# Decoder layer with 64 experts: the shared expert in eleven chunks of rows, and experts and shared expert in one program without a barrier between them

## The reference, cut to what matters

```
logits = x @ gate_weight.T;  topk_w, topk_i = top 6 of 64 experts, from the best 3 of 8 groups
slot   = expert * 192 + position in the expert          # 192 places per expert
g, u   = buf @ Wg.T, buf @ Wu.T                         # 64 experts, 352 inner rows each
yk     = ((silu(g) * u) @ Wd.T)[slot]                   # six rows per token
routed = sum over k of topk_w[k] * yk[k]
shared = (silu(x @ Sg.T) * (x @ Su.T)) @ Sd.T           # 704 inner rows, all tokens
out    = x3 + routed + shared                           # x3: the stream before this block
```

## Time and profile before

| | |
|---|---|
| three runs | 1631.30, 1635.71, 1635.98 us; median 1635.71 us |
| profiled execution | 1641.41 us, span 1639.7 us |
| PE | 1506.2 us busy, 92% of the span |
| DVE, ACT, POOL | 70%, 55%, 47% of the span |
| mean granted clock of PE | 0.957 |
| self and cross attention | up to 670 us |
| expert phase | 670 to 1396 us |
| shared phase | 1396 to 1639.7 us |

### The profile page before, as it was taken

The page is one execution under the profiler, slowest core; times in us unless marked ns, Lnnn a source line. Parts: engine busy times, 40 slices in busy tenths (PEclk is TensorE's granted clock), DMA queues, the critical chain, the costliest instruction groups (busy, mean ns, idle before and its releaser), DMA issues. The chain is left out here.

```text
span 1639.7 us, 30631 instructions
## 1 busy us (share of the span) xinstructions
PE 1506.2 (92%) x10424; PEld 1248.8 (76%) x10424; DVE 1139.9 (70%) x2051; ACT 896.2 (55%) x1765; POOL 766.0 (47%) x957
## 2 busy tenths in 40 slices
PE   4999998989999865499999999999999998799997
PEld 3788886778888754388888888888888886676775
DVE  5677666546888787587777777777777774465655
ACT  3556665644544331287777777777777775312110
POOL 1122234233465555265655565556555653345543
PEclk9999998999999976599999999999999999799999
DMA  6012212321221110698877777788777772436553
GB/s 192 8 59 78 66 47 73 103 75 66 72 76 40 43 49 33 229 328 286 279 265 273 264 267 263 266 282 281 268 272 264 269 263 90 145 117 205 180 165 115
DMA packets 108609, 275.35 MB, mean 168 GB/s; under 512 B 16048, under 2 KB 16048, under 8 KB 108528
## 3 DMA queue, kind: packets, MB, share of 16 engines
q1 hardware_dynamic: 90784, 223.40, 40.2%
q0 software_dynamic: 15360, 50.34, 9.5%
q10 hardware_dynamic: 2384, 0.53, 0.2%
HBM read 232.28 MB, written 41.94 MB: 167 GB/s over the span
## 5 line engine op out<-in xcount | busy, mean ns | idle before, releaser
L2126 POOL TENSOR_TENSOR e_hid<-e_h_raw,e_hid 128x128 fp32r<-128x128 f32 (+1 forms) x192 | 163.9, 854 | 221.3 <-ACT e_hid L2192 221.3
L2350 PE MATMUL e_gu<-e_xT_hi_lo,e_wg 128*128 128x384 f32 (+1 forms) x768 | 231.4, 357 | 1.6 <-issue 1.6
L2350 PE MATMUL e_gu<-e_xT_hi_lo,e_wu 128*128 128x384 f32 (+1 forms) x768 | 230.3, 355 | 0.0
L2352 PE MATMUL e_gu<-e_xT_hi_lo,e_wu 128*128 128x192 f32 (+1 forms) x768 | 193.2, 252 | 0.0
L2352 PE MATMUL e_gu<-e_xT_hi_lo,e_wg 128*128 128x192 f32 (+1 forms) x768 | 193.0, 251 | 0.0
L2134 POOL TENSOR_TENSOR e_wd<-e_raw_d,e_wd 96x512 fp32r<-96x512 f32 x64 | 131.5, 2054 | 36.4 <-ACT e_wd L2177 36.4
L2263 DVE TENSOR_TENSOR e_total<-e_gu,e_low 128x384 f32<-128x384 f32 (+1 forms) x192 | 105.6, 550 | 54.5 <-issue 36.6
L2350 PEld LDWEIGHTS e_gu<-e_xT_hi_lo,e_wg 128*128 128x128 f32 (+1 forms) x768 | 138.0, 180 | 6.9 <-issue 2.6
L2352 PEld LDWEIGHTS e_gu<-e_xT_hi_lo,e_wg 128*128 128x128 f32 (+1 forms) x768 | 139.8, 182 | 1.4
L2350 PEld LDWEIGHTS e_gu<-e_xT_hi_lo,e_wu 128*128 128x128 f32 (+1 forms) x768 | 137.8, 179 | 3.8
L2352 PEld LDWEIGHTS e_gu<-e_xT_hi_lo,e_wu 128*128 128x128 f32 (+1 forms) x768 | 139.6, 182 | 0.0
(11 more groups left out here) (330 smaller groups left out, 4091.2 us busy)
## 6 DMA issues: line engine op xcount, KB each, us to landing
e_raw_g<-in_L_ffn_Wg_dram SPq DMA_DIRECT2D x64, 704.0 KB
e_raw_u<-in_L_ffn_Wu_dram SPq DMA_DIRECT2D x64, 704.0 KB
e_raw_d<-in_L_ffn_Wd_dram SPq DMA_DIRECT2D x64, 512.0 KB, 6.2
y_dram<-e_y_main SPq DMA_DIRECT2D x64, 256.0 KB, 7.9
e_raw_d<-in_L_ffn_Wd_dram SPq DMA_DIRECT2D x64, 192.0 KB, 7.5
y_dram<-e_y_rest SPq DMA_DIRECT2D x64, 128.0 KB, 7.0
a_v<-in_x_dram SPq DMA_DIRECT2D x16, 256.0 KB
s_xr<-in_x_dram SPq DMA_DIRECT2D x16, 256.0 KB
```

The costliest lines, as they stand in the source:

```text
L2126: pool.tensor_tensor(hid[b][1][0:n, c, :], h_raw[g.odd][b][0:n, c, 0:P], hid[b][0][0:n, c, :].bitcast(F32), ALU.subtract).then_inc(s_hl, 1)
L2350: pe.matmul(bank[0:n, 0:2 * CAP], w[b][0][:, k, m:m + n], xT[:, :, k, toks], start=k == 0, stop=False)
L2352: ins = pe.matmul(bank[0:n, 0:CAP], w[b][1][:, k, m:m + n], xT[:, 0, k, toks], start=False, stop=k == KC - 1)
```

## The change

Five things are changed, all in the expert and shared phases.

1. **Chunks.** The 704 inner rows become five full chunks of 128 and one half of 64 (`FULL = 5`, `HALF = 64`). In the sixth chunk the last 64 rows of gate and of up lie side by side in one weight buffer (`h_sg`, 768 columns wide), so that one set of 4 x `matmul3` makes both, gate in rows 0 to 63 of the bank and up in rows 64 to 127. There are 11 such sets instead of 12.
2. **Down.** The hidden values of the half chunk are kept as one buffer, lo part in rows 0 to 63 and hi part in rows 64 to 127; the weights of down likewise. Two matmuls then do what three did: per tile 17 instead of 18.
3. **Wait of down.** For the first tile of a quad, `down` waits chunk by chunk instead of for all.
4. **One program.** `expert_phase` and `shared_phase` become builders of five functions each, and `feed_forward` runs them one behind the other in one block. The barrier, and SP's wait for the last stores, are gone; instead POOL waits for the three stores before its first gather, and other instructions wait for the semaphore that frees their buffer or bank (`free`). The shared expert's buffers lie over expert buffers that are done: the lo weights over the raw ones (in place), the hi weights over the raw buffers of the experts.
5. **Work moved into the last turn.** `load_xf(0)` is issued in the first turn, behind the loads of the shared weights. The splits of the weights of gate and up (11 pieces of 128x512 instead of 8 of 128x704, in the order of use) and of the first tokens go between the last turn's instructions on ACT and DVE, the first 16 transposes between those of PE.

The core of the diff:

```diff
-SCH = ((0, 128), (128, 128), (256, 128), (384, 128), (512, 96), (608, 96))
+FULL = MS // P
+HALF = MS - FULL * P
+SCN = FULL + 1
+INNER = 2 * FULL + 1
@@ expert program, SP
+            ahead.load_xf(sp, 0)
@@ expert program, ACT, in half()
                 if more:
                     gu_hi(*nxt(g, b), 0)
+                else:
+                    ahead.split_hi(act, 0, 2)
...
+                else:
+                    ahead.split_hi(act, 2, 4)
...
-            for b in range(2):
-                main_out(pair(turns - 1), b)
+            ahead.x_hi(act, 0, 0, 2)
+            ahead.split_hi(act, 4, 6)
+            main_out(pair(turns - 1), 0)
+            ahead.x_hi(act, 0, 2, QT)
+            ahead.split_hi(act, 6, INNER)
+            main_out(pair(turns - 1), 1)
@@ expert program, DVE, behind the last half
+            ahead.x_lo(dve, 0, 0, 2)
+            ahead.split_lo(dve, 4, 6)
+            ahead.x_lo(dve, 0, 2, QT)
+            ahead.split_lo(dve, 6, INNER)
             rest_out(pair(turns - 1))
@@ expert program, PE
+                else:
+                    ahead.turn_tokens(pe, 0, 0, 2)
                 down_main(g, 0)
...
+            ahead.turn_tokens(pe, 0, 2, QT)
             down_main(pair(turns - 1), 1)
             down_rest(pair(turns - 1))
@@ shared program, POOL
+            for stored in free["y_stored"]:
+                pool.wait_ge(*stored)
@@ shared program, PE
             def hidden(q, first):
                 pe.wait_ge(s_tl, QT * (q + 1))
-                for c, (m, n) in enumerate(SCH):
+                if first:
+                    pe.wait_ge(*free["gate_up_banks"])
+                for c in range(SCN):
+                    if first:
+                        pe.wait_ge(s_wl, min(2 * c + 2, INNER))
...
-                    for w, bank in ((sg, gt[c % 2]), (su, up[c % 2])):
+                    for w, bank in ((sg, gt[c % 2]), (su, up[c % 2]))[0:2 if c < FULL else 1]:
...
             def down(q, first):
-                pe.wait_ge(s_hl, len(SCH) * (q + 1))
...
+                    for c in range(FULL):
+                        if t == 0:
+                            pe.wait_ge(s_hl, SCN * q + c + 1)
+                        matmul3(pe, bank[:], (hid[0][:, c, toks], hid[1][:, c, toks]), (sd[0][:, c, :], sd[1][:, c, :]),
+                                c == 0, False)
+                    if t == 0:
+                        pe.wait_ge(s_hl, SCN * (q + 1))
+                    pe.matmul(bank[:], hid_half[:, toks], sd[1][:, FULL, :], start=False, stop=False)
+                    pe.matmul(bank[:], hid_half[high_rows, toks], sd[0][high_rows, FULL, :], start=False, stop=True
+                              ).then_inc(s_dn, 1)
@@ feed_forward, one block
+        @block.tensor
+        def _(pe):
+            experts.pe(pe)
+            shared.pe(pe)
```

More of the change, by code:

```diff
@@ L2404, in _, with shared_buffers, sb, shared_programs @@
             turn(pair(turns - 1), False, True)
+            ahead.turn_tokens(pe, 0, 2, QT)
             down_main(pair(turns - 1), 1)
             down_rest(pair(turns - 1))
-def shared_phase(nc, raw, loaded, xf, x3, y_in, out, weight, slot, ident):
+        mine.sync, mine.pool, mine.act, mine.dve, mine.pe = sync, gpsimd, scalar, vector, tensor
+    return mine
+def shared_buffers(nc, ctx):
+    def sb(name, shape, dt=F32):
+        return ctx.enter_context(nc.sbuf_tensor("h_" + name, shape, dt))
+    return dict(xf=sb("xf", [P, QT, H]), ones=sb("ones", [P, 1]),
+                idx=[sb(f"idx{b}", [P, TOPK], U32) for b in range(2)], w_t=[sb(f"w_t{b}", [P, TOPK]) for b in range(2)],
+                carry=[sb(f"carry{b}", [P, 1]) for b in range(2)])
+def shared_programs(nc, sems, mine, own, raw, loaded, xf, x3, y_in, out, weight, slot, ident, experts):
     quads = BATCH // QT
@@ L2620, in turn @@
                         routed(q, early, range(3 * ((c - 1) % 2), 3 * ((c - 1) % 2) + 3))
-                hidden_lo(q, len(SCH) - 1, first)
+                hidden_lo(q, FULL, first)
                 if not last:
-                    x_lo(q + 1)
+                    x_lo(dve, q + 1, 0, QT)
                 for t in range(QT):
@@ L2691, in _, with feed_forward @@
             turn(quads - 1, False, True)
+        mine.load_xf, mine.split_hi, mine.split_lo = load_xf, split_hi, split_lo
+        mine.x_hi, mine.x_lo, mine.turn_tokens = x_hi, x_lo, turn_tokens
+        mine.sync, mine.pool, mine.act, mine.dve, mine.pe = sync, gpsimd, scalar, vector, tensor
+def feed_forward(nc, wg_in, wu_in, wd_in, shared_in, xf, x3, table, y, out, weight, slot, ident):
+    with ExitStack() as ctx:
+        sems = []
+        raw = []
+        own = shared_buffers(nc, ctx)
+        loaded = nc.alloc_semaphore("shared_weights_loaded")
+        sems.append(loaded)
+        shared = Programs()
+        experts = expert_programs(nc, sems, wg_in, wu_in, wd_in, xf, table, y, ident, shared_in, raw, loaded, shared)
+        shared_programs(nc, sems, shared, own, raw, loaded, xf, x3, y, out, weight, slot, ident, experts)
+        ctx.callback(end_phase, nc, sems)
+        block = ctx.enter_context(nc.Block())
+        @block.sync
+        def _(sp):
+            experts.sync(sp)
+            shared.sync(sp)
+        @block.gpsimd
+        def _(pool):
+            experts.pool(pool)
+            shared.pool(pool)
+        @block.scalar
+        def _(act):
+            experts.act(act)
+            shared.act(act)
+        @block.vector
+        def _(dve):
+            experts.dve(dve)
+            shared.dve(dve)
+        @block.tensor
+        def _(pe):
+            experts.pe(pe)
+            shared.pe(pe)
 _INS = ['x', 'ctx_2048', 'mask_BxS2_ik0', 'L0_attn_Wqkv', 'L0_attn_bqkv', 'L0_attn_Wo', 'L0_attn_bo', 'L0_xattn_Wq',
```

276 lines of the change are left out of this document (146 added, 130 removed).

## The result

| | before | after |
|---|---|---|
| median of four runs each, same chip | 1635.85 us | 1609.32 us (1608.08 to 1611.85) |
| ratio | | 0.9839, interval [0.9806, 0.9871] |
| profiled execution | 1641.41 us, span 1639.7 | 1611.85 us, span 1610.2 |
| TensorE's mean granted clock | 0.957 | 0.963 |

What follows compares the result with a forecast made beforehand. PE bounds the expert turns and nearly all of the shared phase, with a break between them. Terms 16.25 + 2.5 + 11.7 + 1.8 - 1.6 + 4.85 = 35.5 us give 1600.2, stated as 1600.5; range 1595 to 1609 (0.8).

Steps and rivals of the forecast that it cites:

- The seam: From the experts' last gate_up to the first shared-expert matmul: that matmul starts at 1391.5 instead of 1407.75, saving 16.25 us.
- the clock in quad 0: Start of quad 0: the first 12 matmuls run at clock 1.00 instead of 0.50, saving 2.5 us.
- 1.5 us that the text had kept for the range: In the seam: extra gain if the clock does not fall during down_main and down_rest; left out of the sum.
- Eleven chunks: Gate and up of each quad: 36 matmuls replace 48 in the last chunks, saving 2.93 us a quad, 11.7 in four.
- Down: Down stage: one matmul less per tile saves 0.92 us a quad, counting in quads 1 and 2, 1.8 us.
- The short last chunk: End of gate and up: DVE gives x_lo later, PE waits 0.8 us longer in quads 1 and 2, -1.6 us.
- Quad 1's wait for DVE: In quad 1: PE comes earlier and its wait for DVE grows from 0.95 to 1.9 us.
- The last quad: Quad 3: down begins on ready chunks, finish of tile 1 8.1 us after the last silu instead of 12.95; 4.85 us.
- The tail behind it stays: After finish of tile 1 in the last quad: the last routed sums and store, 14.9 us, remain unchanged.
- The start: Turn 1 of the experts: 1 MB loaded ahead of its weights costs 0, bounds 0 and 3.2 us.
- The first (clock and ACT give some back, 1603 to 1608): Quad 1 and start: falling clock, late silu and late weights cost 2 to 7 us; chance 0.20.
- Its rule from the Trainium skill: Quad 1's loop: branches to unheld instructions wait for a fetch, so late silus return in looping programs; sum then 1602.

Runs made afterwards that it cites:

- full_rows: The changed kernel with the half chunk's second down matmul on 128 rows, the lower 64 of its weights zero; 1607.24 us, 0.9826 of before.
- unrolled: all_quads with the loops over the quads written out on PE, ACT and DVE; 1593.85 us, 0.9737 of before.
- all_quads: combined with the token transposes behind the first two down tiles in quad 0 too; 1590.14 us, 0.972 of before.
- before_64: The kernel before with its inner rows cut as five chunks of 128 and one of 64, nothing else; 1636.39 us, 0.9983 of before.
- trios_early: The changed kernel with the groups of three routed sums behind chunks 0 to 3 instead of 1 to 4; 1605.36 us, 0.98 of before.
- x3_first: The changed kernel with SP asking for residual rows before it stores the output tile; 1608.56 us, 0.9805 of before.
- combined: The changed kernel with zero-padded half-chunk down, earlier routed sums, residual rows first, transposes behind down tiles in quads 1 and 2; 1594.27 us, 0.973.
- nothing_moved: The changed kernel with the shared expert's splits and token transposes behind the experts' last instructions, still one program; 1624.67 us, 0.9918 of before.

## Why the prediction was right in sign and 9 us short

- **The seam (16.25; measured 16.9) and the clock in quad 0 (2.5).** Right, with their mechanism: `h_gt` at 1389.70, no wait above 1.25 in the last turn, `hidden` of quad 0 30.1 us (1389.70 to 1419.76) where 29.9 were named. That the size came so near is in part luck. The clock stayed up through `down_main` and `e_dn_rest`, 1.5 us that the text had kept for the range. And the second `down_main` started 6.7 us behind `gate_up`'s end instead of 5.7, waiting for POOL, whose last hidden piece took 1.60 us where it took 0.45 before.
- **Eleven chunks (2.93 a quad).** Right. From the first `h_gt` of a quad to the end of `hidden`, quads 1 and 2 took 34.1 and 32.9 us before and 31.2 and 30.1 after.
- **Down: the step that failed.** It said that one matmul less per tile saves 0.92 us a quad, 1.8 us in all, and rested on "by these rows its height changes nothing". But in those rows of gate and up, 96 is the number of columns of the weights (128*96), and the height is 128 throughout; the only matmuls of another height in the rows are the 96 high ones within the 4.14 us of a `down` tile. None was 64 high. From its first matmul to the next quad's, `down` went from 18.2 and 17.7 us in quads 1 and 2 to 19.1 and 18.9: a loss of 2.1 in place of the gain. With 128 rows (full_rows) it is 16.8 and 17.5, a gain of 1.4 and 0.2, together near the 1.8. The term's sign was wrong by the price of two changes of height, 0.40 us a tile: eight tiles, 3.2 of the 3.9 us between forecast and result. Most of the rest lies in quad 2, where more matmuls than before ran at the lower clock (six starts 0.43 apart, four before).
- **The short last chunk (-1.6).** Right as a mechanism, too small. From the first transpose to the first `h_dn` took 4.85 and 5.02 before, 6.36 and 5.77 after: -2.3. The wait is 3.71 where 3.3 to 3.6 were named, the clock falls behind it in both quads as it did before (in quad 1; 0.50 over 1561 to 1563 in quad 2), and in quad 0, which the forecast left out, the stretch grew too (4.91 to 5.35).
- **Quad 1's wait for DVE.** 1.9 was named, 0.85 measured: PE did not come earlier, since `down` was not shorter. In full_rows, where it is, the wait is 1.87, so the reasoning was right and failed with the step above.
- **The last quad (4.85; measured 3.9).** `finish` of tile 1 at S3 + 9.03 instead of 8.1; full_rows has 8.45, so 0.6 of the 0.9 goes away with the height.
- **"The tail behind it stays" was wrong by 1.5 us**: 0.99 for the residual rows, the rest mostly the last store (4.2 us from the last `finish` to the end, 3.9 before).
- **The start (0).** Right in the sum. ACT waits 3.05 us in turn 1, but for `e_raw_g`, and 0.72 for `e_raw_d`, which had been named with 2 or 3; PE does not wait (busy for 60.00 of the 60 us from 700 to 760).
- **The rivals.** The first (clock and ACT give some back, 1603 to 1608) lies nearest to the result in size, but not by its means: no late silu and no start cost appeared. Its rule from the Trainium skill (Runtime: NRT & Kernel Launch, Instruction fetch mechanics) read as "returns in each program that loops" is not borne out: the profiled execution of after loops and has no late silu, and unrolled, without the loops, has one 1.0 us late in quad 0 as all_quads has; no run here shows a fetch by itself. The range was too narrow by a price that no row showed: the half-height matmul had no row, and should have had bounds.

## What to carry to other kernels

Keep all matmuls of a stream at one height: pad a half-height block with zero weights rather than change height, here worth 0.4 us a tile (in the tile's own stretch; the whole kernel did not get measurably faster by it alone). When a chunk is made shorter, walk the other engines' work through it, since what hid under 5.4 us of matmuls may not fit under 2.7. Transposes for the next block belong behind the first tiles of the long matmul stage, not in front of it, where TensorE waits and then works on at half its clock: moving them was worth 5.9 and 5.1 us in the two quads where TensorE sets the pace, and nothing that shows in quad 0, where VectorE does. And before a wait without a named releaser is taken for something unknown, look what the other engines ended just before it: here it was a product on VectorE.

## What was not expected of the hardware

- Two changes of height in TensorE's stream cost about 0.4 us together (0.40 after, 0.37 a tile in before_64), in upper and lower rows alike; going from 128 to 96 rows cost nothing (0.23 a matmul), and from 128 to 64 columns in gate and up neither (0.22 in before_64).
- After the same wait of 2.70 us for `x_lo` in trios_early the granted clock stayed at 1.00 in quad 1 (2.4 GHz) and fell to 0.50 (1.2 GHz) in quads 0 and 2 (over 1422 to 1424 and 1528 to 1530); after 3.71 us it fell to 0.50 in both quads of after.
- ACT's silus in quads 0 and 1 start up to 7.5 us after the matmuls that they wait for (x3_first; about 5 in full_rows, two of them), at different chunks in different kernels. Behind quad 1 it is rare: 3.5 us once in quad 2 of combined, which lengthened nothing (S1 to S2 47.51, as in all_quads). In full_rows, x3_first and nothing_moved, where it comes in quad 1 at 5 us or more, S0 to S1 is 57.65 to 58.08 us instead of 54.56. The cause is open.
